# Scores and values product of two pairs of heads at a time in a one-core transformer kernel

## What is computed

```python
x = x + attn_a(layernorm(x))    # 16 heads of 64, bias by relative position, softmax over 256 keys
x = x + experts(layernorm(x))   # 8 experts, 128 -> 512 -> 128, relu, the one best expert of each token, times its gate
x = x + attn_b(layernorm(x))    # causal over the 256 tokens of a batch;
                                # keys and values from a latent of rank 128
x = x + experts(layernorm(x))
```

## Time and profile before

| | |
|---|---|
| Timed runs | 758.76, 760.29, 761.10 us (median 760.29) |
| Profiled execution | 753.58 us, span 752.3 us |
| PE / PE weight load busy | 710.9 us (95%) / 562.9 us (75%) |
| ACT / DVE / POOL busy | 556.9 (74%) / 498.4 (66%) / 369.9 us (49%) |
| Granted TensorE clock, mean | 0.989 |
| DMA | 45.71 MB, most of it in the first 190 us |

### The profile page before, as it was taken

The page is one execution under the profiler, slowest core; times in us unless marked ns, Lnnn a source line. Parts: engine busy times, 40 slices in busy tenths (PEclk is TensorE's granted clock), DMA queues, the critical chain, the costliest instruction groups (busy, mean ns, idle before and its releaser), DMA issues. The chain is left out here.

```text
span 752.3 us, 18939 instructions
## 1 busy us (share of the span) xinstructions
PE 710.9 (95%) x5568; PEld 562.9 (75%) x5568; DVE 498.4 (66%) x2203; ACT 556.9 (74%) x1872; POOL 369.9 (49%) x675
## 2 busy tenths in 40 slices
PE   4999999999999999898899999999999999989894
PEld 4767777777777777588897777777777777768794
DVE  3876767676767677835756667786677767955633
ACT  3887878787878787835767878787787879765552
POOL 2454545654565355515754344456446535625643
PEclk9999999999999999989999999999999999999998
DMA  9899899960000000231220000000000000120122
GB/s 265 152 185 183 166 268 175 182 98 3 2 15 2 1 2 16 58 118 37 63 62 18 1 3 2 1 3 15 2 2 16 2 1 1 34 52 24 49 75 78
DMA packets 77205, 45.71 MB, mean 61 GB/s; under 512 B 8422, under 2 KB 74361, under 8 KB 76849
## 3 DMA queue, kind: packets, MB, share of 16 engines
q1 hardware_dynamic: 72000, 39.22, 27.4%
q0 software_dynamic: 2944, 4.23, 1.9%
q10 hardware_dynamic: 2160, 1.05, 0.6%
HBM read 18.34 MB, written 27.97 MB: 62 GB/s over the span
## 5 line engine op out<-in xcount | busy, mean ns | idle before, releaser
L287 POOL TENSOR_SCALAR ring<-ring,rs 128x256 f32<-128x256 f32 (+1 forms) x500 | 220.8, 459 | 233.4 <-DVE rs L1042 232.4
L762 ACT ACTIVATE ring<-ring,mn 128x256 f32<-128x256 f32 (+1 forms) x512 | 240.8, 482 | 0.0
L468 PE MATMUL ps<-qk 64*128 64x256 f32 (+1 forms) x1024 | 131.9, 376 | 0.7 <-DVE mn L1031 0.6
L502 PE MATMUL ps<-pt,v 128*64 128x256 f32 (+1 forms) x1024 | 126.0, 367 | 6.3 <-DVE pt L1058 4.3
L377 PE MATMUL ps<-ident,ring 128*128 128x128 f32 x896 | 121.0, 275 | 2.2 <-POOL ring L287 2.0
L730 ACT COPY qk<-ps 128x512 f32<-128x512 f32 x128 | 75.0, 586 | 55.2 <-PE ps L374 54.4
L377 PEld LDWEIGHTS ps<-ident,ring 128*128 128x128 f32 x896 | 102.0, 141 | 14.0 <-POOL ring L287 5.6
L502 PEld LDWEIGHTS ps<-pt,v 128*64 128x64 f32 x1024 | 63.5, 136 | 60.4 <-issue 27.3
L762 ACT ACTIVATION_READ_ACCUMULATOR ring<-ring,mn 128x1 f32 x512 | 101.4, 198 | 0.0
L468 PEld LDWEIGHTS ps<-qk 64*128 64x128 f32 x1024 | 77.8, 186 | 26.1 <-issue 13.8
L294 POOL DMA_INDIRECT ys_scratch<-f_ys,f_xs x60 | 62.9, 1048 | 67.1 <-DVE f_ys L1162 57.7
(11 more groups left out here) (178 smaller groups left out, 1333.6 us busy)
## 6 DMA issues: line engine op xcount, KB each, us to landing
xs_scratch<-padt SPq DMA_DIRECT2D x16, 1032.0 KB, 18.9
w<-in_W SPq DMA_DIRECT2D x16, 256.0 KB, 5.6
xs_scratch<-padt SPq DMA_DIRECT2D x4, 967.5 KB, 18.7
f_xs<-xs_scratch SPq DMA_DIRECT2D x60, 64.5 KB, 1.8
T<-in_bias SPq DMA_DIRECT2D x1, 1536.0 KB, 14.2
xn<-ys_scratch SPq DMA_DIRECT2D x6, 256.0 KB, 3.9
bu<-in_w_kv_up SPq DMA_DIRECT2D x1, 1024.0 KB, 7.1
ys_scratch<-f_ys,f_xs POOLq DMA_INDIRECT x60, 2.3
```

Source lines behind the costliest of these rows:

```text
L287: i = pool.tensor_scalar(ring[:, hh, it, 0:w], ring[:, hh, it, 0:w], rs[:, q], 1.0, ALU.mult, ALU.mult)
L468: i = pe.matmul(PS[hh][:, 256 * it:256 * it + w], qk[rows, 128 * it:128 * it + 128], qk[rows, 256:256 + w], start=True, stop=True)
L502: i = pe.matmul(PO[64 * hh:64 * hh + 64, lo:256], a_v[b % 2][:, jt, 128 * c + 64 * hh:128 * c + 64 * hh + 64], a_pt[(U0 + u) % 2][:, hh, 2 ...
L762: i = act.activation(ring[:, hh, it, 0:w], ring[:, hh, it, 0:w], ACT.Exp, bias=mn[:, q], scale=-1.0, accum_out=sm[:, q])
```

## The change

- PE computes the scores of two units together, in odd steps: `S(s-1)` and `S(s)`, and the values product of two units together, also in odd steps: `PV(s-5)` and `PV(s-4)`. In even steps there is neither.
- The scores have four banks: 1 and 2 for even units, 3 and 7 for odd ones. `claim` waits until a bank's last user is through. Other uses take banks 1 and 2 in even steps of the attention, and 3 and 7 in odd ones and later.
- The values product of an odd unit goes to the upper half of bank 6. `keep` takes two units in one instruction of 512 columns, in even steps.
- pre_b, pre_c, out_2 and post_b, post_c, post_d (`after`) move ahead of TR in PE's and ACT's step, pre_b, pre_c and out_2 also in DVE's; the sums of the norm behind out_2 (`sums`) stay behind DVE's `S`. `out` stays behind TR.
- The waits on `a_o` and `v_o` count pairs. The two transposes of the output weights move from steps 3 and 4 to 2 and 4.

POOL's program is unchanged. In DVE's, `weigh(s-3)` still follows the copy of `TR(s-4)` and precedes `S(s-1)`.

```diff
@@ -49,7 +49,7 @@
 BLOCKS = [[(k, min(16, r // 128 - k)) for k in range(0, r // 128, 16)] for r in XROWS]
 FILLS = [16 * len(b) for b in BLOCKS]
 D_W = 5 + 2 * NE
-LAST = {NU + 1: (0, 1, 2, 3), NU + 2: (4,), NU + 3: (5,), NU + 4: (6, 7)}
+LAST = {NU + 1: (0, 1, 2, 3), NU + 2: (4, 5), NU + 4: (6, 7)}

...
@@ -104,7 +104,7 @@

     ps = [ctx.enter_context(nc.psum_tensor(f"ps{i}", [128, 512], F32)) for i in range(8)]
     PT_ = ps[0]
-    PS = ps[1:3]
+    PS = [(ps[1], ps[2]), (ps[3], ps[7])]
     PP = ps[4:6]
     PO = ps[6]

...
@@ -356,17 +357,22 @@
                 steps[1](s - OFF)


-    turn, held = [3], {3: None, 7: None}
-
-    def spare(use, done, n, bank=None):
-
-        if bank is None:
-            turn[0] = bank = 10 - turn[0]
+    free_in, held = [(3, 7)], {0: None, 1: (v_m, 2), 2: (v_m, 3), 3: (v_m, 4), 7: None}
+
+    def claim(bank, done, n):
+
         if held[bank]:
             pe.wait_ge(*held[bank])
         held[bank] = (done, n)
+        return ps[bank]
+
+    def spare(use, done, n, bank=None):
+
+        if bank is None:
+            bank, other = free_in[0]
+            free_in[0] = (other, bank)
         bank_of[use] = bank
-        return ps[bank]
+        return claim(bank, done, n)

     def three(out, ah, al, bh, bl, first=True, last=True):
         pe.matmul(out, ah, bh, start=first, stop=False)
...
@@ -399,7 +405,7 @@
         kH, kL = (a_lth, a_ltl) if st else (a_xth, a_xtl)

         def pre_b(b):
-            PX = spare(("x", B0 + b), v_x, B0 + b + 1)
+            PX = spare(("x", B0 + b), v_x, B0 + b + 1, None if B0 + b else 7)
             pe.wait_ge(v_xh, B0 + b + 1)
             for j in range(2):
                 i = tr(PX[:, 128 * j:128 * j + 128], a_xh[:, j, :])
...
@@ -459,13 +465,13 @@
         def S(u):
             qk = a_qk[(U0 + u) % 2]
             pe.wait_ge(a_t, U0 + u + 1)
-            if U0 + u:
-                pe.wait_ge(v_mn, 2 * (U0 + u))
+            for hh, bank in enumerate(((1, 2), (3, 7))[u % 2]):
+                claim(bank, v_mn, 2 * (U0 + u) + hh + 1)
             for it in range(2):
                 w = 128 if causal and it == 0 else 256
                 for hh in range(2):
                     rows = slice(64 * hh, 64 * hh + 64)
-                    i = pe.matmul(PS[hh][:, 256 * it:256 * it + w], qk[rows, 128 * it:128 * it + 128],
+                    i = pe.matmul(PS[u % 2][hh][:, 256 * it:256 * it + w], qk[rows, 128 * it:128 * it + 128],
                                   qk[rows, 256:256 + w], start=True, stop=True)
             i.then_inc(t_s, 1)

...
@@ -494,12 +500,13 @@
                 pe.wait_ge(v_fy, NF)
             if c == 0:
                 pe.wait_ge(a_vs, 4 * B0 + VALUE_NO[(b, 3)] + 1)
-            if U0 + u:
-                pe.wait_ge(v_o, U0 + u)
+            if U0 + u and u % 2 == 0:
+                pe.wait_ge(v_o, (U0 + u) // 2)
+            col = 256 * (u % 2)
             for jt in range(2):
                 lo = 128 if causal and jt == 1 else 0
                 for hh in range(2):
-                    i = pe.matmul(PO[64 * hh:64 * hh + 64, lo:256],
+                    i = pe.matmul(PO[64 * hh:64 * hh + 64, col + lo:col + 256],
                                   a_v[b % 2][:, jt, 128 * c + 64 * hh:128 * c + 64 * hh + 64],
                                   a_pt[(U0 + u) % 2][:, hh, 256 * jt + lo:256 * jt + 256], start=(jt == 0), stop=(jt == 1))
             i.then_inc(t_pv, 1)
...
@@ -511,8 +518,8 @@

         def out(b):
             PX = spare(("o", B0 + b), a_oTs, 7 * st + b + 1)
-            pe.wait_ge(a_o, U0 + 8 * b + 8)
-            pe.wait_ge(v_o, U0 + 8 * b + 8)
+            pe.wait_ge(a_o, (U0 + 8 * b + 8) // 2)
+            pe.wait_ge(v_o, (U0 + 8 * b + 8) // 2)
             out_weights(b)
             for c in range(8):
                 i = three(PX[:, 0:256], wo[:, c, 0:128], wo[:, c, 128:256], a_oh[:, c, :], a_ol[:, c, :],
...
@@ -594,8 +601,8 @@
             if j == 0:
                 pe.wait_ge(a_fx, NG * st + g + 1)
             pe.wait_ge(v_fw, NF * st + n + 1)
-            if n < 2:
-                pe.wait_ge(v_mn, 2 * (U0 + NU))
+            if n < 20:
+                claim(1 + n % 2, a_fr, NF * st + n + 1)
             else:
                 pe.wait_ge(a_fr, NF * st + n - 1)
             for f in range(4):
...
@@ -633,25 +640,30 @@

         def step(s):
             n = s - F0
+            free_in[0] = (1, 2) if s < NU and s % 2 == 0 else (3, 7)
             if 0 <= s < NU:
                 QK(s)
             if s in VALUES:
                 values(*VALUES[s])
+            if (b := pre_at(s, "b", st)) is not None:
+                pre_b(b)
+            if st and (b := pre_at(s, "c", st)) is not None:
+                pre_c(b)
+            if (b := at(s, 13)) is not None and b < NB - 1:
+                out_2(b)
+            if s < NU:
+                after(s)
             if 4 <= s < NU + 4:
                 TR(s - 4)
             if 0 <= n < NF:
                 H(n)
-            if 1 <= s <= NU:
-                S(s - 1)
-            if (b := pre_at(s, "b", st)) is not None:
-                pre_b(b)
-            if st and (b := pre_at(s, "c", st)) is not None:
-                pre_c(b)
             if (b := at(s, 12)) is not None and b < NB - 1:
                 out(b)
-            if (b := at(s, 13)) is not None and b < NB - 1:
-                out_2(b)
-            if 4 <= s < NU + 4:
+            if s % 2 and 1 <= s < NU:
+                S(s - 1)
+                S(s)
+            if s % 2 and 5 <= s < NU + 4:
+                PV(s - 5)
                 PV(s - 4)
             if 2 <= n < NF + 2:
                 Y(n - 2)
...
@@ -660,6 +672,11 @@
             for g in range(NG):
                 if n == max(GROUPS[g][0] - 2, -1):
                     XT(g)
+            if s >= NU:
+                after(s)
+
+        def after(s):
+
             if (b := post_at(s, "b")) is not None:
                 post_b(b)
             if (b := post_at(s, "c")) is not None:
...
@@ -715,13 +732,14 @@
             act_high(a_lth[b % 2][:, :], ps[bank_of[("l", b)]][:, 0:256], a_l)

         def keep(u):
+
             b, c = divmod(u, 8)
-            act.wait_ge(t_pv, U0 + u + 1)
+            act.wait_ge(t_pv, U0 + u + 2)
             if c == 0 and b:
                 act.wait_ge(t_out, 7 * st + b)
             elif c == 0 and st:
                 act.wait_ge(t_last, 1)
-            act_high(a_oh[:, c, :], PO[:, 0:256], a_o)
+            act_high(a_oh[:, c:c + 2, :].rearrange("p c n -> p (c n)"), PO[:, :], a_o)

         def T(u):
             act.wait_ge(t_t, U0 + u + 1)
...
@@ -849,20 +867,22 @@
             n = s - F0
             if NU < s < NU + 2:
                 expo(s - 2)
-            if 5 <= s < NU + 5:
-                keep(s - 5)
+            if s % 2 == 0 and 6 <= s < NU + 5:
+                keep(s - 6)
             if 0 <= s < NU:
                 T(s)
             if s in VALUES:
                 values(*VALUES[s])
+            if (b := pre_at(s, "b", st)) is not None:
+                pre_b(b)
+            if st and (b := pre_at(s, "c", st)) is not None:
+                pre_c(b)
+            if s < NU:
+                after(s)
             if 4 <= s < NU + 4:
                 TR(s - 4)
             if 2 <= s <= NU:
                 expo(s - 2)
-            if (b := pre_at(s, "b", st)) is not None:
-                pre_b(b)
-            if st and (b := pre_at(s, "c", st)) is not None:
-                pre_c(b)
             if (b := at(s, 12)) is not None and b < NB - 1:
                 out(b)
             if 0 <= n < NF:
...
@@ -1003,7 +1028,8 @@

         def keep(u):
             c = u % 8
-            low(a_ol[:, c, :], PO[:, 0:256], a_oh[:, c, :], a_o, U0 + u + 1, v_o)
+            low(a_ol[:, c:c + 2, :].rearrange("p c n -> p (c n)"), PO[:, :],
+                a_oh[:, c:c + 2, :].rearrange("p c n -> p (c n)"), a_o, (U0 + u + 2) // 2, v_o)

         def S(u):
             c = u % 8
...
@@ -1021,7 +1047,7 @@
             if st and u == 0:
                 dve.wait_ge(p_set, k["cm"])
             for hh in range(2):
-                bank = PS[hh]
+                bank = PS[u % 2][hh]
                 if hh == 0:
                     dve.wait_ge(t_s, U0 + u + 1)
                 if U >= 3:
...
@@ -1076,8 +1102,10 @@
             dve.wait_ge(t_o2, 7 * st + b + 1)
             dve.tensor_tensor(xx, ps[bank_of[("o2", B0 + b)]][:, 0:256].rearrange("p (a d) -> p a d", a=2), xx,
                               ALU.add).then_inc(v_res, 1)
+
+        def sums(b):
             dve.wait_ge(v_res, B0 + b + 1)
-            norm_a(xx, s2, m2, r2, v_var1)
+            norm_a(x[:, 2 * b:2 * b + 2, :], s2, m2, r2, v_var1)

         def post_a(b):
             xx = x[:, 2 * b:2 * b + 2, :]
...
@@ -1204,24 +1232,28 @@
                 start_rows(0)
             if NU < s < NU + 3:
                 weigh(s - 3)
-            if 5 <= s < NU + 5:
-                keep(s - 5)
```

(37 more changed lines are left out.)

## The result

The changed kernel takes 811.95 us (median of 4 runs, 808.47 to 817.43), the kernel before beside it 760.6: ratio 1.0686, 95% interval 1.0609 to 1.0764. It is 51 us slower. The forecast was 785, 25 us slower; the time lies outside the range of 768 to 803.

What follows compares the result with a forecast made beforehand. The prediction took attention as bound twice, by PE and by the loop, 0.07 us apart. Stage 0 +18.8, stage 1 +5.5, in all +24.3, and +1 for the rest: +25 on 760.3 gives 785 us, range 768 to 803.

Steps and rivals of the forecast that it cites:

- the loop: Attention: TR, DVE's copy and reciprocal, POOL's multiplication, next TR can't go round under 3.86 us, 3.33 in stage 1.
- Rival 1: Faster: POOL's result comes before PE wants it, 48 loop-bound gaps shrink, about -50 in place of +25: 711; chance 0.07.
- The layouts: PE in attention: two units together pay layout passages once; second S and second PV cost 0.86 us each, 0.65 in stage 1.
- rival 2: A second block of the same layout pays its passages again, 0.35 us in 60 odd-to-even gaps: +21, 806; chance 0.06.
- PE busy lower by some 45 us: Sign that the forecast is right: PE's busy time falls by some 45 us.
- Gaps at residues 4 and 6: Even-to-odd TR, step modulo 8: 4 filled by output projection, 4.62 and 4.74 us; 6 waits for DVE's norm, 4.0 and 3.5.
- Gaps at residue 0 with late counts: Batches 1, 3 and 5: tile counts ahead of TR need the choice of expert, 5.0 us, 4.5 in stage 1.
- The collision at bank 3: Bank 3, first choice in late steps, also belongs to the expert inputs: one collision a stage, about 0.5 to 1 us.
- start, tail and expert stretches: Outside the attention gaps: +1 us for all of it, with -3 and +4 as bounds.
- So I price the clock at nothing: Attention: PE stays busy about 87%, a stretch with 8.00 of 10 us busy kept clock 1.00, so no clock cost.
- The fourth rival: The clock falls: one stretch, 3.5 us lost, in each of 15 rounds of eight steps: +52, 837; chance 0.07.
- Borrowed banks: Odd steps' first value projection waits for DVE's reduction, ends about 3.2 us, under the loop's 3.86: costed at nothing.

Runs made afterwards that it cites:

- experiment 2: Changed kernel with the reciprocal first in DVE's step, ahead of the copy of TR: 778.2 us, ratio 1.0265 to the kernel before.
- experiment 3: Kernel before with the same edit, the reciprocal first in DVE's step: 754.0 us, ratio 0.9946.
- experiment 6: Changed kernel with the odd step's four blocks in the order S, PV, S, PV: 836.3 us, ratio 1.1013 to the kernel before.
- experiment 5: Changed kernel with the reciprocal first in DVE's step and the late counts one step later: 772.5 us, ratio 1.0159 to the kernel before.
- experiment 7: On top of experiment 5, value projections only in even steps, router's blocks behind TR in odd ones: 756.2 us, ratio 0.9948 to the kernel before.
- experiment 8: On experiment 7, router's transposes and logits a step later, DVE's logits addition ahead of its reductions: 737.4 us twice, ratios 0.9865 and 0.9849 to before.
- experiment 1: Changed kernel with the counts of rows by expert one step later, behind the choice: 797.1 us, ratio 1.0499 to the kernel before.
- experiment 9: On top of experiment 8, ACT copies the odd unit's projections ahead of the even step's exponentials: 807.0 us, ratio 1.0780 to the kernel before.

## Why the prediction was wrong

The direction held, and so did most of the gap model. The size failed on the clock first of all. The profiled run lies 38.5 us over the sum (63.8 against 25.3). The clock inside the attentions has up to 19 of them by estimate, start and expert stretches 11 (12 against 1), two terms of the gaps 8 and a collision at a bank 4; that is more than 38.5, because the clock's share is an upper bound.

*What bounds the kernel, and the loop.* Right, and shown by experiments 2 and 3. (Rival 1's "48 loop-bound gaps" are, by the list of gaps itself, 28 bound by the loop, 14 by the norm and 6 by the counts.) The loop-bound gaps measured 3.85 to 3.88 us (forecast 3.86) and 3.34 to 3.38 (3.33).

*The layouts.* Right: experiment 6 gives the 0.35 us of rival 2's row. The odd-to-even gaps were 5.65 and 4.58 us (5.58 and 4.52); where TR doesn't wait (experiments 2, 5, 7) they are 5.58 and 4.53, so the 0.07 goes with a TR behind a wait, x 60 some 4 us that the sum lacks. "PE busy lower by some 45 us" was too much: it is 714.8 against 710.9 us, with the matmuls at half clock in it, and in experiment 8's kernel, at full clock in both attentions, 508.3 against 538.9 there, 31 lower.

*Gaps at residues 4 and 6.* 4.68 and 4.79 (4.62, 4.74); 4.28 and 3.77 (4.0, 3.5). The latter was mis-sized by 0.27: 14 times, 4 us. The rows of TR at 171.70 (next TR at 175.98) show of what it consists:

```profile
174.82 0.77 DVE L958 TENSOR_SCALAR ph<-x,m,r 128x128 f32<-128x128 f32 x2
```
```profile
175.73 0.41 PE L383 MATMUL ps<-ident,ph 128*128 128x128 f32 x2 [0.50 <-DVE ph L958]
175.98 1.04 PE L383 MATMUL ps<-ident,ring 128*128 128x128 f32 x8
```

The reductions end where forecast (3.12 us behind TR, 3.13), the norm's pair takes 0.77 us and not 0.60, waking PE 0.14 and not 0.1, and the transposes 0.25 and not 0.19.

*Gaps at residue 0 with late counts.* 4.62 us in attention 1 (4.5). In attention 0 5.5, because the clock fell inside it (5.0; experiment 2, at full clock, has 4.92 to 4.97).

*The collision at bank 3.* The sum had it within the +1 for start, tail and expert stretches, "at about 0.5 to 1 us". It stands in the last gap of each attention (unit 60 to 61), where the transposes of the expert inputs wait for the scores' bank:

```profile
356.00 0.66 PE L383 MATMUL ps<-ident,f_xs 128*128 128x128 f32 x4 [2.64 <-DVE mn L1057]
```

These gaps take 5.95 and 5.57 us where 3.86 and 3.33 were forecast, 2.1 and 2.2 more. It isn't mainly the clock: in experiment 1 the same wait is 2.64 us again, at full clock, and the gaps take 5.94 and 5.36.

*"So I price the clock at nothing".* This is the step that failed. I had argued from the mean share of busy time (87%, against a stretch with 8.00 of 10 us at full clock), and the clock fell where two waits meet: the value projection's wait for its bank and the wait for the choice together leave PE 2.11 us of work in 4. I had priced both waits at nothing beyond the gap. Each time it costs 2.8 us in the gap behind and some 0.5 in its own, at units 21, 37 and 53 of attention 0; the half-clock stretches in the start and at its end come on top. The clock column puts 0.05 x 326.55 / 0.5 = 33 us of attention 0 at 1.2 GHz; at full clock PE would have done that work in about half, so up to 16 us of the 39.3. With the 18.8 forecast, the 4 us of two terms above (0.07 x 30 and 0.27 x 7) and the 2 of the collision, that is the stage to within 2 us. In attention 1 it is 2.7 of 12.5. Experiment 1 took 15 us by moving two small matmuls and nothing else. That shows the idle ahead of the counts to be needed for these stretches; experiment 2, where 1.73 us of it in place of 1.89 mostly left the clock at 1.00, shows that it isn't enough by itself, and what else it takes stays open. The Trainium skill, page "TensorE: Matmul & The Clock Gate", section "A second HAM failure mode: psum-queue depth-cycling", has the clock swing from short idles between matmul groups; the trace agrees that it can fall in such a loop and not in its manner: some 40 short stalls of 1.1 to 1.5 us left it at 1.00, a few longer ones didn't. The fourth rival, with chance 0.07, had the right mechanism; it put one stretch in each of 15 rounds, and some eight were seen, two in the start and six inside the attentions.

*Borrowed banks.* "Under the loop's 3.86" was right in the plain pairs, where the wait shows (0.83 us) and costs nothing; experiment 2 uncovers it, experiments 5 and 7 remove it for 16 us with the router's blocks. In the start it was not covered. There DVE also has the output weights and the bias table ahead of its reductions, the third value projection waits 2.38 us, TR of unit 0 comes 4.3 us later, and two half-clock stretches lie there. That the 2.38 us bring the clock down isn't shown: experiment 5 has the same wait at a clock of 1.00. I had put +1 on start, tail and experts, with +4 as bound; they gave +12.

*The expert stretches,* +3.9 us each. The clock (0.95 against 0.96, 0.91 against 0.94) makes up some 1 and 3 us of it, by the same estimate. The rest stays open.

*Spread.* The runs reach from 808.5 to 817.4, those of before from 758.8 to 761.1. The executions with spans of 807.2 and 816.1 us differ in their mean clock, 0.969 and 0.959: 0.010 x 812 / 0.5 is 16 us at half clock, 8 us of time. So the same idle seems to bring the clock down in one execution and not in another; only the trace of the longer one is there, so this is read from the means and not shown place by place.

## What to carry to other kernels

When work is taken out from between two steps of a chain that runs over several engines, first write down what the chain takes from start to start, and compare it with what is left on the busy engine in each gap by itself, not with the mean of the two. The mean busy share was no guide to TensorE's clock here: it fell first where two waits met. Price the clock with a range, because nearly the same idle gave either outcome. The gain of pairing was real here, and it could be had (1.4% faster than before) once what the pair needs of the other engines was asked for earlier or needed later: the reciprocal, the bank, the counts, the norm.

## What the runs showed of the hardware

- Two more passages between a 64-row and a 64-column block of matmuls cost 0.35 us together (6.00 against 5.65 us from TR to TR over the same four blocks, experiment 6).
- The clock stayed down for longer than the idle ahead of it lasted: 2.11 us of work in 4, and then 6.8 us at half clock. The stalls of 1.1 to 1.5 us in every pair left the clock at 1.00 (experiment 1). Nearly the same idle left it at 1.00 at five of six places of experiment 2 (2.27 us of work in 4 at the first). In experiment 9, with one wait of some 3 us a batch, it fell in nearly every batch.
- The same kernel before had medians of 758.0 to 760.6 us in three sets of runs and of 748.3 and 748.8 us on two other chips, 1.3 to 1.6% apart, so that times from different chips are compared only by ratio.
